# Field-pair projection: three stores a tile in place of four, five in the first tile and four in the last

## The chip, the cores and the metric

The kernel runs on one core of one Trainium2 chip. The time is that of one execution on the device, in microseconds (us). The kernel before took 684.77 us (median of three runs, 684.7 to 685.42).

## The reference

Every sample has 32 fields of 64 numbers. For each of the 496 pairs of fields (i, j) with i < j, field i is projected by the pair's own 64 x 64 matrix and multiplied, element by element, with field j:

```
r_x: (2048, 32, 64) float32      W: (496, 64, 64) float32
PAIRS = list(combinations(range(32), 2))
proj = einsum('bpd,pod->bpo', x[:, pi, :], W)
y    = proj * x[:, pj, :]        # (2048, 496, 64) float32
```

The output is 260 MB, the weights are 8 MB and x is 17 MB: it is above all a kernel that writes.

## The kernel before

The batch is cut into 16 tiles of 128 samples, one sample on each partition. The weights stay in SBUF from the start. For a tile, x is loaded into one of two buffers (`x_sb`), "turned" on TensorE (16 transposes into PSUM, which ScalarE copies to `x_t`), and then taken through 21 steps. A step has two halves (an even field i and an odd one), and each half is up to 1,024 columns, that is 16 pairs: TensorE multiplies the turned field with the weights into PSUM (`project`, line 294). Then VectorE multiplies PSUM with field j into the buffer `staged` (line 338). In the steps named in `pool_steps` (two of three) the second half goes another way: ScalarE copies PSUM into `staged` (line 260) and GpSimd multiplies it there with field j in place (line 221). PSUM holds two steps (`proj`, two buffers).

The steps of a tile form 11 groups of consecutive pairs: 61, 57, 53, 49, 45, 41, 37, 33, 54, 38 and 28 pairs. Groups 0 to 7 have two steps each (0 to 15), group 8 has steps 16 and 17, group 9 has 18 and 19, group 10 has step 20. The turn of the *next* tile's x stands between steps 9 and 10 (`TURN_BEFORE`); the last tile has none. `MERGED` says which groups share one *slot* of `staged` and one store. A slot exists once: the next tile may write into it when its store has landed. That is `slot_free` (line 163): VectorE waits ahead of the slot's first step, ScalarE ahead of the slot's first step with its work. All stores are issued by SyncE (SP), in order, each as soon as its last group is computed (lines 173 to 192); they run on queue q1, as do the loads of the weights and the first two x tiles. In the first and the last tile every group is stored by itself, 11 stores.

The x of tile t + 1 is loaded during tile t, by ScalarE's queue (q10): `load_x` (line 239) stands ahead of step 3 in ScalarE's order, behind the ScalarE copies of steps 0 and 1. It waits until all of tile t - 1 is computed, since that tile used the same buffer. TensorE waits for this load at the turn (line 302).

Each store writes one contiguous row per partition: 256 bytes a pair, so 30,208, 26,112, 31,488 and 39,168 bytes in the four stores of an inner tile. Sixteen DMA engines share the 128 partitions, 8 rows to each, and each engine ends a transfer with a small write to the semaphore. In the profile such a row is one packet.

Of the kernel before, what the change touches and what calls it, by code (L numbers as in the profile page):

```python
# [13 lines left out]
LOAD_BEFORE = 3  # L14
WARM_UP = 16

MERGED = [[0, 1], [2, 3], [4, 5, 6], [7, 8, 9, 10]]

DMA_SCRATCH = 1024

# [1 line left out]
def pair_index(i, j, fields):  # L22

    return i * (2 * fields - i - 1) // 2 + (j - i - 1)


def plan(fields, dim):


    fit = UNIT // dim  # L30
    steps, groups = [], []
    for i in range(0, fields // 2, 2):
        cut = fit if fields - 1 - i > fit + fit // 2 else fit // 2
        groups.append([len(steps), len(steps) + 1])
        steps.append(([(i, i + 1, cut)], [(i + 1, i + 2, cut)]))
        steps.append(([(i, i + 1 + cut, fields - 1 - i - cut)], [(i + 1, i + 2 + cut, fields - 2 - i - cut)]))

    def whole(*of):
        return [(i, i + 1, fields - 1 - i) for i in of]
    groups += [[len(steps), len(steps) + 1], [len(steps) + 2, len(steps) + 3], [len(steps) + 4]]  # L40
    steps += [(whole(16), whole(17)), (whole(18), whole(19)), (whole(20), whole(21)), (whole(22), whole(23)),
              (whole(24, 30, 26, 28), whole(25, 29, 27))]
    return steps, groups
# [30 lines left out]
def field_pair_project(nc, x, w, ident, out, fields, dim):  # L74
    batch = x.shape[0]
    tiles = batch // P
    steps, groups = plan(fields, dim)
# [10 lines left out]
    def items(tile):  # L88


        for n, item in enumerate(last_tile if tile.last else whole_tile):
            yield item, (1 + n) % 2, tile.number * per_tile + (1 + n) // 2
# [5 lines left out]
    def group_range(g):  # L98
        segments = [seg for s in groups[g] for unit in steps[s] for seg in unit]
        first = min(pair_index(i, j, fields) for i, j, _ in segments)  # L100
        assert sum(n for _, _, n in segments) == max(
            pair_index(i, j, fields) + n for i, j, n in segments) - first
        return first, sum(n for _, _, n in segments)


    slot_of = [next(k for k, merged in enumerate(MERGED) if g in merged) for g in range(len(groups))]
    slots = len(MERGED)
    slot_range = [(group_range(m[0])[0], sum(group_range(g)[1] for g in m)) for m in MERGED]


# [9 lines left out]
    def every_tile(emit):  # L120

        for t in range(tiles):
            emit(Tile(t, t % 2, t // 2, last=t == tiles - 1))
# [9 lines left out]
    with ExitStack() as ctx:  # L133
# [3 lines left out]
        def sem(name):  # L137
            return ctx.enter_context(nc.semaphore(name))
# [5 lines left out]
        x_t = [sb(f"x_t{h}", [P, fields // 2, P]) for h in range(2)]  # L144
        ident_sb = sb("ident_sb", [P, P])
        staged = [sb(f"staged{k}", [P, n * dim]) for k, (_, n) in enumerate(slot_range)]

        proj = [[ctx.enter_context(nc.psum_tensor(f"proj{b}{h}", [P, UNIT], F32)) for h in range(2)]
# [10 lines left out]
        stored = [sem(f"stored{k}") for k in range(slots)]  # L159
# [3 lines left out]
        def slot_free(eng, tile, k):  # L163

            if not tile.first:
                eng.wait_ge(stored[k], 16 * (tile.number + len(MERGED[k]) - 1))

        def staged_part(s, i, j, n):
            k = slot_of[group_of[s]]
# [3 lines left out]
        @block.sync  # L173
        def _(sp):
            def emit(tile):
                where = {item: (b, use) for item, b, use in items(tile)}
                fine = tile.first or tile.last
                for these in [[g] for g in range(len(groups))] if fine else MERGED:
                    k, g = slot_of[these[0]], these[-1]
                    first, n = group_range(these[0])[0], sum(group_range(h)[1] for h in these)  # L180


                    pooled = [h for h in these if any(s in pool_steps for s in groups[h])]
                    if pooled and these[0] == 0:
                        sp.wait_ge(pool_scaled[pooled[-1]], tile.number + 1)
                    b, use = where[groups[g][-1]]
                    sp.wait_ge(emptied[b][groups[g][-1] not in pool_steps], use + 1)
                    if pooled and these[0] > 0:
                        sp.wait_ge(pool_scaled[pooled[-1]], tile.number + 1)
                    at = (first - slot_range[k][0]) * dim  # L190
                    sp.dma_start(out[bass.ds(tile.number * P, P), first * dim:(first + n) * dim],
                                 staged[k][:, at:at + n * dim]).then_inc(stored[k], 16)

            half = fields * dim // 2
            sp.dma_start(x_sb[0][:, 0:half], x[0:P, 0:half]).then_inc(x_first_loaded[0], 16)  # L195
            sp.dma_start(w_sb[:, w_cuts[0]:w_cuts[1]], w[:, w_cuts[0]:w_cuts[1]]).then_inc(w_loaded[0], 16)  # L196
            sp.dma_start(x_sb[0][:, half:], x[0:P, half:]).then_inc(x_first_loaded[1], 16)  # L197
            for c in range(1, len(w_cuts) - 2):
                sp.dma_start(w_sb[:, w_cuts[c]:w_cuts[c + 1]], w[:, w_cuts[c]:w_cuts[c + 1]]  # L199
                             ).then_inc(w_loaded[c], 16)  # L200

            c = len(w_cuts) - 2
            sp.dma_start(w_sb[0:dim, w_cuts[c]:w_cuts[c + 1]], w[0:dim, w_cuts[c]:w_cuts[c + 1]]  # L203
                         ).then_inc(w_loaded[c], 16)
            sp.dma_start(x_sb[1][:], x[P:2 * P, :]).then_inc(x_loaded[1], 16)

            every_tile(emit)
            for k in range(slots):
                sp.wait_ge(stored[k], 16 * (tiles - 2 + 2 * len(MERGED[k])))

        @block.gpsimd
        def _(pool):
# [17 lines left out]
        def _(act):  # L230
# [17 lines left out]
            def emit(tile):  # L248
                for item, b, use in items(tile):
                    if item == LOAD_BEFORE and not tile.first and not tile.last:  # L250
                        load_x(tile)
                    if item == "turn":
                        turned_out(b, use, 1 - tile.parity)
                    elif item in pool_steps:
                        (i, j, n), = steps[item][1]
                        k = slot_of[group_of[item]]
                        if item == min(s for s in pool_steps if slot_of[group_of[s]] == k):
                            slot_free(act, tile, k)
                        act.wait_ge(filled[b][1], use + 1)  # L259
                        nc.scalar.activation(staged_part(item, i, j, n), proj[b][1][:, 0:n * dim],  # L260
                                             ACT.Copy).then_inc(emptied[b][1], 1)
# [58 lines left out]
        @block.vector  # L320
        def _(dve):
            def emit(tile):
                if tile.first:
                    for h in range(2):
                        dve.wait_ge(x_first_loaded[h], 16)
                for item, b, use in items(tile):
                    if item == "turn":
                        continue
                    k = slot_of[group_of[item]]
                    if item == groups[MERGED[k][0]][0]:  # L330
                        slot_free(dve, tile, k)
                    for h in range(2):
                        if h and item in pool_steps:
                            continue
                        dve.wait_ge(filled[b][h], use + 1)
                        segments = steps[item][h]
                        for (i, j, n), at in zip(segments, place(segments, dim)):
                            last = nc.vector.tensor_tensor(  # L338
                                staged_part(item, i, j, n), proj[b][h][:, at:at + n * dim],
                                x_sb[tile.parity][:, j * dim:(j + n) * dim], ALU.mult)  # L340
                        last.then_inc(emptied[b][h], 1)

            every_tile(emit)
# [31 lines left out]
```

## Time and profile before

| what | value |
|---|---|
| median of 3 runs | 684.77 us |
| the profiled execution | 684.55 us, span 682.7 us, mean granted clock 0.919 |
| busy: PE, DVE, ACT, POOL | 573.4, 409.3, 208.4, 391.9 us |
| HBM read, written | 24.97 MB, 260.05 MB: 417 GB/s over the span |
| stores | 14 each of 4896, 3936, 3776 and 3264 KB; 22 of 896 to 1952 KB |
| x loads on ScalarE's queue | 14 of 1024 KB, median 17.8 us to landing |
| chain that ended last | PE 55%, DMA 37% (all of it x loads) |

The page cuts the span into 40 slices of 17 us. The mean busy share of the 16 DMA engines is 90% or more in all of them but the first and the last; PE is at 90% or more in most, too, and none of its work is left in the last two slices. PE is TensorE, DVE is VectorE, ACT is ScalarE, POOL is GpSimd and SP is SyncE; "SPq" and "ACTq" are the queues from which the two issue DMAs. Times in rows count from the start of the span. A mean busy share can come out a little over 1, since a packet's time is counted where it starts.

### The profile page before, as it was taken

To read this page: it belongs to the slowest core of one execution; us is meant where nothing else is said; L and a number is where in the kernel's file an instruction comes from. 1 tells how busy PE (TensorE), PEld (TensorE's weight loads), DVE (VectorE), ACT (ScalarE), POOL (GpSimd) and SP (SyncE) were. 2 spreads that over 40 slices of the span, in tenths; PEclk is the share of its full clock that TensorE was granted. 3 is DMA by queue.
4 is the path that set the end of the run, shared out by engine and by line. 5 is a ranking of instruction groups with operands and counts; after the bars stand their busy time and mean duration, and the time that the engine had idled before them with its cause. 6 is when DMAs were issued, how large, how long until landed. Compare 5 with 4: busy or idle time off the path is not lost.

```text
span 682.7 us, 7003 instructions
## 1 busy us (share of the span) xinstructions
PE 573.4 (84%) x2704; PEld 363.3 (53%) x2704; DVE 409.3 (60%) x528; ACT 208.4 (31%) x257; POOL 391.9 (57%) x228
## 2 busy tenths in 40 slices
PE   6899989979799796988969889697996979979930
PEld 4565646546465564645646456464654646546520
DVE  1677775837567473764837638386583756837730
ACT  3334333323233333332323323233332323332300
POOL 1768674646566374674646836468464665647720
PEclk9999999989899898998989989899898989989975
DMA  8999999999999999999999999999999999999995
GB/s 336 386 426 425 439 438 423 434 436 428 432 432 431 432 428 436 435 427 428 431 427 429 428 404 410 428 421 407 426 426 424 422 415 429 399 439 419 421 421 233
DMA packets 15648, 285.20 MB, mean 418 GB/s; under 512 B 1744, under 2 KB 1872, under 8 KB 3856
## 3 DMA queue, kind: packets, MB, share of 16 engines
q1 hardware_dynamic: 13472, 270.28, 93.3%
q10 hardware_dynamic: 2160, 14.75, 5.1%
q8 instruction: 5, 0.08, 0.0%
q14 instruction: 11, 0.09, 0.0%
HBM read 24.97 MB, written 260.05 MB: 417 GB/s over the span
## 4 chain that ended last, share of the span: by engine, by line
PE 55%; DMA 37%; DVE 2%; SPq 1%; issue 1%; ACT 0%; DVEq 0%; ACTq 0%
PE proj L294 47%; DMA x_sb<-x_dram 37%; PE proj L272 7%; DVE staged L338 2%; SPq L199 1%; ACT staged L260 0%; SPq L203 0%; SPq L197 0%; SPq L196 0%; SPq L195 0%; DVEq L133 0%; ACTq L259 0%
## 5 line engine op out<-in xcount | busy, mean ns | idle before, releaser
L338 DVE TENSOR_TENSOR staged<-proj,x_sb 128x1024 f32<-128x1024 f32 (+7 forms) x528 | 409.3, 826 | 246.5 <-PE proj L294 210.8
L221 POOL TENSOR_TENSOR staged<-staged,x_sb 128x1024 f32<-128x1024 f32 (+4 forms) x224 | 391.7, 1755 | 261.4 <-ACT staged L260 258.4
L294 PE MATMUL proj<-w_sb,x_t 64*128 64x512 f32 (+7 forms) x2432 | 518.7, 533 | 3.6 <-DVE staged L338 2.1
L294 PEld LDWEIGHTS proj<-w_sb,x_t 64*128 64x128 f32 x2432 | 313.1, 188 | 204.3 <-issue 121.6
L260 ACT ACTIVATE staged<-proj 128x1024 f32<-128x1024 f32 (+4 forms) x224 | 174.6, 787 | 356.5 <-PE proj L294 329.1
L272 PE MATMUL proj<-ident_sb,x_sb 128*128 128x128 f32 x256 | 52.6, 390 | 71.2 <-DMA x_sb<-x_dram 71.2
L272 PEld LDWEIGHTS proj<-ident_sb,x_sb 128*128 128x128 f32 x256 | 47.1, 208 | 80.3 <-DMA x_sb<-x_dram 79.8
L236 ACT ACTIVATE x_t<-proj 128x1024 f32<-128x1024 f32 x32 | 32.5, 1024 | 86.2 <-PE proj L272 86.1
L311 PE MATMUL proj<-ident_sb 128*128 128x128 f32 x16 | 3.4, 405 | 5.6 <-DMA ident_sb<-ident_dram 5.6
L311 PEld LDWEIGHTS proj<-ident_sb 128*128 128x128 f32 x16 | 3.2, 223 | 5.6 <-DMA ident_sb<-ident_dram 5.6
L236 ACT ACT_TABLE_LOAD x1 | 1.3, 1283 | 1.2 <-PEq L368 1.2
L368 POOL MEMSET const-float32-0.0<- 128x1 f32 x1 | 0.1, 99 | 0.2 <-issue 0.2
L368 POOL MEMSET const-bfloat16-1.0<- 128x1 bf16 x1 | 0.1, 102 | 0.0
L368 POOL MEMSET const-uint8-127<- 128x1 uint8 x1 | 0.1, 102 | 0.0
L368 POOL MEMSET const-float32-1.0<- 128x1 f32 x1 | 0.1, 99 | 0.0
## 6 DMA issues: line engine op xcount, KB each, us to landing
out_dram<-staged SPq DMA_DIRECT2D x14, 4896.0 KB, 26.0
out_dram<-staged SPq DMA_DIRECT2D x14, 3936.0 KB, 23.0
out_dram<-staged SPq DMA_DIRECT2D x14, 3776.0 KB, 27.7
out_dram<-staged SPq DMA_DIRECT2D x14, 3264.0 KB, 27.7
x_sb<-x_dram ACTq DMA_DIRECT2D x14, 1024.0 KB, 17.8
out_dram<-staged SPq DMA_DIRECT2D x2, 1952.0 KB, 16.8
out_dram<-staged SPq DMA_DIRECT2D x2, 1824.0 KB, 20.6
out_dram<-staged SPq DMA_DIRECT2D x2, 1728.0 KB, 21.8
```

Of the source, the lines that this page charges most:

```text
L199: sp.dma_start(w_sb[:, w_cuts[c]:w_cuts[c + 1]], w[:, w_cuts[c]:w_cuts[c + 1]]).then_inc(w_loaded[c], 16)
L221: last = nc.gpsimd.tensor_tensor(product, product, x_sb[tile.parity][:, j * dim:(j + n) * dim], ALU.mult)
L236: nc.scalar.activation(x_t[to][:, h * (UNIT // P):(h + 1) * (UNIT // P), :].rearrange("p k b -> p (k b)"), proj[b][h][:], ACT.Copy).then_i ...
L260: nc.scalar.activation(staged_part(item, i, j, n), proj[b][1][:, 0:n * dim], ACT.Copy).then_inc(emptied[b][1], 1)
L272: last = nc.tensor.transpose(proj[b][h][:, n * P:(n + 1) * P], x_sb[of][:, k * P:(k + 1) * P], ident_sb[:])
L294: last = nc.tensor.matmul(proj[b][h][:, at:at + width], x_t[tile.parity][half, i // 2, :], w_sb[half, col:col + width], start=True, stop=True)
L311: nc.tensor.transpose(proj[1][0][:, 0:P], ident_sb[:], ident_sb[:])
L338: last = nc.vector.tensor_tensor(staged_part(item, i, j, n), proj[b][h][:, at:at + n * dim], x_sb[tile.parity][:, j * dim:(j + n) * dim], ...
L368: nc = bacc.Bacc("TRN2", target_bir_lowering=False, num_devices=1, dynamic_dma_scratch_size=DMA_SCRATCH)
```

## The change

Inner tiles are stored in three parts in place of four: groups 0 to 2 (171 pairs, 43,776 bytes a row), 3 to 6 (172 pairs, 44,032 bytes) and 7 to 10 (153 pairs, 39,168 bytes, as before). The slots of `staged` are cut in the same way, with the same size in sum. The first tile has five stores, of 61, 110, 94, 78 and 153 pairs. The last tile has four, of 171, 172, 87 and 66 pairs. The counts on the semaphores that say when a slot is free follow from how many stores of the first tile go to it. Steps, loads and their places in every engine's order stay.

```diff
-MERGED = [[0, 1], [2, 3], [4, 5, 6], [7, 8, 9, 10]]
+MERGED = [[0, 1, 2], [3, 4, 5, 6], [7, 8, 9, 10]]
+FIRST_MERGED = [[0], [1, 2], [3, 4], [5, 6], [7, 8, 9, 10]]
+LAST_MERGED = [[0, 1, 2], [3, 4, 5, 6], [7, 8], [9, 10]]
...
+    def stores_of(merged, k):
+
+        return sum(slot_of[these[0]] == k for these in merged)
+
...
             if not tile.first:
-                eng.wait_ge(stored[k], 16 * (tile.number + len(MERGED[k]) - 1))
+                eng.wait_ge(stored[k], 16 * (tile.number - 1 + stores_of(FIRST_MERGED, k)))
...
-                fine = tile.first or tile.last
-                for these in [[g] for g in range(len(groups))] if fine else MERGED:
+                for these in FIRST_MERGED if tile.first else LAST_MERGED if tile.last else MERGED:
...
             for k in range(slots):
-                sp.wait_ge(stored[k], 16 * (tiles - 2 + 2 * len(MERGED[k])))
+                sp.wait_ge(stored[k], 16 * (tiles - 2 + stores_of(FIRST_MERGED, k) + stores_of(LAST_MERGED, k)))
```

## Rows read from the trace of the kernel before

**Rows 1.** The page, DMA: packets and bytes; then q1's packets, MB, share.
```profile
DMA packets 15648, 285.20 MB, mean 418 GB/s; under 512 B 1744, under 2 KB 1872, under 8 KB 3856
...
q1 hardware_dynamic: 13472, 270.28, 93.3%
```

**Rows 2.** Windows: us; busy of PE, PEld, DVE, ACT, POOL; clock; DMA share, GB/s.
```profile
103.42:602.43 499.01, 431.92 (x2016) 273.83 (x2017) 306.76 (x396) 155.65 (x192) 293.80 (x168) 0.92 1.00 425
...
614.30:615.10 0.80, 0.80 (x8) 0.66 (x6) 0.02 (x2) 0.19 (x1) 0.54 (x1) 1.00 0.17 65
...
673.00:674.00 1.00, 0.00 (x0) 0.00 (x0) 0.00 (x0) 0.00 (x0) 0.00 (x0) 0.50 1.04 434
...
676.00:682.00 6.00, 0.00 (x0) 0.00 (x0) 0.00 (x0) 0.00 (x0) 0.00 (x0) 0.50 0.06 25
```

**Rows 3.** The chain of waits, in order of time: start, us, what.
```profile
103.42 2.95 PE proj L272 x16
...
143.69 3.67 PE proj L272 x16
...
309.98 3.68 PE proj L272 x16
...
318.33 9.19 PE proj L294 x36
...
520.37 3.67 PE proj L272 x16
...
561.26 3.67 PE proj L272 x16
...
584.59 17.79 DMA x_sb<-x_dram
...
602.43 3.67 PE proj L272 x16
...
609.67 9.19 PE proj L294 x36
```

**Rows 4.** Waits from 103.42 to 602.43: us in total, times, longest.
```profile
PE proj L272 <- DMA x_sb<-x_dram: 63.5, 12, 6.7
...
DVE staged L338 <- DMA out_dram<-staged: 29.7, 7, 5.6
```

**Rows 5.** DMA queues from 103.42 to 602.43: packets, MB, share of 16 engines.
```profile
q1 hardware_dynamic: 7055, 199.51, 93.7%
q10 hardware_dynamic: 1728, 12.58, 6.0%
```

**Rows 6.** Timeline of SP, ACT and POOL: start, us, engine, line, what, count.
```profile
52.83 0.33 ACTq L245 DMA_DIRECT2D x_sb<-x_dram  x1
...
573.21 0.33 SPq L191 DMA_DIRECT2D out_dram<-staged  x1
...
582.70 0.33 SPq L191 DMA_DIRECT2D out_dram<-staged  x1
...
590.26 0.33 SPq L191 DMA_DIRECT2D out_dram<-staged  x1
...
591.47 2.36 POOL L221 TENSOR_TENSOR staged<-staged,x_sb 128x1024 f32<-128x1024 f32 x1 [1.23 <-ACT staged L260]
...
593.46 1.02 ACT L260 ACTIVATE staged<-proj 128x1024 f32<-128x1024 f32 x1 [2.07 <-PE proj L294]
```

**Rows 7.** DMA queues from 592 to 596, amid an x load.
```profile
q1 hardware_dynamic: 32, 1.25, 79.3%
q10 hardware_dynamic: 32, 0.26, 15.5%
```

**Rows 8.** DMA queue q10 from 588 to 589.7 (none from 584.59 to 588).
```profile
q10 hardware_dynamic: 2, 0.02, 2.3%
```

**Rows 9.** DMA queue q1 from 597.5 to 601.5, the end of that x load.
```profile
q1 hardware_dynamic: 47, 1.44, 83.2%
```

**Rows 10.** The line of the x loads (L245), its 14 loads.
```profile
DMA to landing us min/median/max: 9.3/17.8/19.2
```

## The prediction

> **What bounds the kernel now.** I read the page's DMA lines first, because every engine has slack. They move 285 MB at a mean of 418 GB/s, and q1, with all the stores, holds them for 93.3% of the span [rows 1]. Then the windows: over the twelve inner tiles from 103.42 to 602.43 the mean share of the DMA engines is 1.00 at 425 GB/s, while TensorE (PE) is busy for 432 of 499 us [rows 2]. So the DMA engines are the wall. The end tells more. Up to 674 us all of them move data (434 GB/s), and from 676 to 682 the share is 0.06: one engine of sixteen is still at work, 7 us behind the others [rows 2]. All engines carry the same rows, so that engine is simply slower, and the run lasts as long as *its* rows last. It matters whether it ever pauses.
>
> The chain of waits shows the second limit. In every inner tile it goes from the x load (17.8 us) through the turn on PE and the later steps to the next x load [rows 3]. This loop took 41.17 us in the last inner tile and 41.03 a tile in the last two (602.43 - 520.37 = 82.06). 41.0 is also what I take as the slowest engine's own time for one tile, since it shows no pause before the end. In those late tiles the other fifteen already pause: in the 0.8 us from 614.30, behind the issue of a middle store, the share is 0.17 [rows 2]. PE waits for x 63.5 us in twelve tiles, against 29.7 us that VectorE waits for a store to free its slot [rows 4]. Two limits within 0.2 us of each other, then: the bytes, and the x loop. Anything that makes x later by more than that costs time.
>
> **The change, part by part.**
>
> *Fewer, longer rows.* A store sends one row per partition, 8 to each engine, and a semaphore write. Inner tiles go from 4 stores to 3 (14 fewer), the first tile from 11 to 5, the last from 11 to 4: 27 fewer, 27 x 9 = 243 packets of each engine's 978 (15,648 / 16) [rows 1]. What is one worth? q1 moved 199.51 MB in 93.7% of 16 x 499.01 us, 26.7 KB/us an engine; q10, with rows of 8,192 bytes, 12.58 MB in 6.0%, 26.3 KB/us [rows 5]. On 8,192 bytes that is 5 ns a packet: 243 x 5 ns = 1.2 us saved. Bounds: nothing below; above, if the slow engine's 7 us over its 978 packets were also a price per packet (7 ns more), 3.0 us. I take 1.2.
>
> *Slots.* Slot 0 now frees when the last of steps 0 to 5 has landed, slot 1 covers steps 6 to 13, slot 2 is as before. The slots' waits stand ahead of VectorE's and ScalarE's step, and behind them wait PE (two PSUM buffers) and the x load, which ScalarE issues ahead of step 3. Take one late tile. The middle store is issued at 573.21, the last at 582.70, x at 584.59 [rows 6]. A row of 172 pairs is 44,032 bytes, 1.65 us at 26.7 KB/us, so the new middle store lasts 13.2 us and lands some 15 us after 573.21, at about 588; its slot is wanted by step 6, which ScalarE copies at 593.46 [rows 6]. The first store (13.1 us) follows the last one and lands at about 617; its slot is wanted by step 0 of the next tile, just ahead of the next x issue, at about 624. Five us or more to spare: no wait. The first store becomes ready when GpSimd has finished step 4, 591.47 + 2.36 = 593.8 instead of 590.26 [rows 6]; the engines turn to it after the last store, at about 601. Covered by 7 us; without this cover each late us would be a pause.
>
> *The x load.* This is the part with a price. While x is loading, the engines take one row of a store, one row of x: between 592 and 596, 32 and 32 packets [rows 7]. So x, 8 rows an engine, lands after the 8 store rows that it is mixed with, and how long these are decides.
> The Trainium skill says the same in DMA: Bandwidth & Descriptors, section Queues, rings and completion order: an engine alternates between the queues' rings and drains a whole packet of one before it turns to the other. The trace agrees, and a packet here is one row.
> Now: the middle store (8 rows of 31,488) reaches the engines 0.8 us after its issue, then come 8 rows of 39,168. x is issued 11.38 us after the middle store; the engines take its first 2 rows between 588 and 589.7, 3.4 to 5.1 us after, and the others then [rows 3, 6, 8]. Hence it mixes with the second half of the last store and with 3 rows (30,208) of the next first store (47 packets of q1 on 16 engines, 1.44 MB) [rows 9], and lands 29.17 us after the middle store's issue (584.59 + 17.79 - 573.21). Bytes of stores ahead of x on one engine: 251.9 + 313.3 + 90.6 = 655.8 KB.
> After: the middle store starts at +0.8 and lasts 13.2, to +14.0; x's rows can begin at 11.38 + 3.5 = +14.9. So one row of the last store passes, x mixes with the other seven, and its eighth row follows that store's eighth; no row of the next store need pass. 352.3 + 313.3 = 665.6 KB, 9.8 KB more, 0.37 us. x lands at about 29.55. The step from the turn to the middle store's issue, 11.95 us (573.21 - 561.26), stays: the same steps 10 to 13. The loop becomes 41.5 us. It can be 1 us more where PE's granted clock is at its lower level for longer: turn and first matmuls took 8.35 us from 309.98 but 7.24 from 602.43 [rows 3].
> The slowest engine needs 41.0 for its rows. It falls behind by some 0.8 us a tile at first (the others made 40.27 from 103.42 to 143.69 [rows 3]), about 2 us in the first tiles, an estimate; that feeds it for some three of the 13 loads, and for the other ten it pauses 0.55 each (41.5 and the saved 0.05): 5.5 us. Bounds for the place of x: one row earlier (it slips in ahead of the last store, with 1.8 us less) the loop is 39.7 and costs nothing; one row later (a row of 43,776 passes before x's last) it is 43.1.
>
> *Tile 1.* The load there, issued at 52.83, takes 9.3 us [rows 6, 10], since it lies among rows of 8 to 14 KB. After the change the rows of 39,168 are on: 3.5 + 8 x (1.47 + 0.31) = 17.7, so the turn is at 70.5 and the middle store issued at 82.4. By then the engines have to move 33.1 MB (weights and three x tiles 11.3, tile 0 16.25, the first store 5.6), 79 us at 418 GB/s and a start of some 4: they are busy until 83. Cost none, but this cover is used up.
>
> *The end.* After the last turn no x load is in the way, and 821 pairs a partition remain from the middle store on, some 64 us on the slowest engine. Without a turn the last tile's steps run ahead of the engines, as now: from 673 to 674 PE is long idle and the engines are at 1.04 [rows 2]. Nothing lost.
>
> **Sum.** The profiled execution took 684.55 (span 682.7 and 1.85 around it), 0.22 below the median of 684.77. Median - 1.2 + 5.5 = 689.1; I say 689.0.
>
> **Rivals.** (1) *x slips in a row earlier.* Where the slow engine's lag at the middle store is between 0.3 and 2 us, x's first row passes ahead of the last store and the loop falls below the engine's 41.0. For it: the lag starts near 2, by the estimate above. Against: each tile whose loop is over 41.0 eats it. Time 684.8 - 1.2 = 683.6, with a few short pauses up to 686. (2) *Faster: packets cost more than I think.* The slow engine's lag is a price per packet, not per byte: 3.0 us saved, no pause, 681.8. It decides if a packet costs over 6 ns. For it: the rows give no other reason why one engine is slower. Against: 26.3 against 26.7 KB/us [rows 5] leaves no more than 5 ns on the average engine.
> The Trainium skill goes further in DMA: Bandwidth & Descriptors, section Anatomy of one DMA: about 2.0 us of fixed cost a transfer. By that alone 27 stores would be 54 us; it is an estimate from the page, and the share of 1.00 [rows 2] says that this cost lies beside other stores here (chance 0.01, within rival 2).
> (3) *x a row later.* Loop 43.1, 2.1 over 41.0, in 13 tiles 27 us: 711. Against: x's rows have 1 us to spare.
>
> **How the numbers follow.** Forecast 0.45 (686 to 697: 0.2 to 1.1 us a tile); rival 1 0.30; rival 2 0.12; rival 3 0.13. A measurement of this kernel can tell 0.2%, 1.4 us. Faster: rival 2 and a fifth of rival 1, 0.18. Same (683.4 to 686.1): the rest of rival 1 and a tenth of the forecast, 0.28. Slower 0.54. The range 681.5 to 699 leaves out rival 3 and half of rival 2.
>
> **What would show it.** Right: the x loads' median goes from 17.8 to 18 or more; the twelve turns lie over 41.3 us apart; the mean share over inner tiles falls below 1.00; the lonely engine's tail at the end shrinks from 7 us to 2 or less. The first x load takes about 17 us. Wrong: the tail stays and the turns lie 41.0 apart (rival 1), the DMA share stays 1.00 and the GB/s rise (rival 2), or the x loads take 20 us (rival 3). A wait of VectorE for a slot in every tile would break the part on slots.

## The result and the profile after

The changed kernel takes 709.81 us (median of six runs, 708.18 to 712.56); the kernel before, run beside it, 684.51 (683.84 to 685.42). The ratio is 1.0374, with a 95% interval of 1.035 to 1.0399: 25.3 us slower. Ratios here and below leave out executions over 1.5% above the fastest of the same kernel; only f1 and f3 had such, two of ten each. The forecast, 689.0, had the sign; the time lies outside its range and next to rival 3 (711).

The page after: packets of all queues; the x loads (KB, median us from issue to landing).

```profile
DMA packets 11760, 285.19 MB, mean 404 GB/s; under 512 B 1312, under 2 KB 1440, under 8 KB 3168
...
x_sb<-x_dram ACTq DMA_DIRECT2D x14, 1024.0 KB, 19.3
```

A quarter of the packets is gone [rows 1], and the mean rate fell from 418 to 404 GB/s: the engines pause. The windows after (columns as in rows 2) show where: the inner tiles first, then 2 us of a turn, the stretch just before a middle store's issue, and the end.

```profile
112.51:627.94 515.43, 432.06 (x2017) 273.11 (x2017) 308.31 (x396) 155.54 (x192) 293.60 (x168) 0.91 0.95 403
...
586.00:588.00 2.00, 2.00 (x11) 2.00 (x10) 0.00 (x0) 0.38 (x1) 0.00 (x0) 0.50 0.81 350
...
596.50:598.05 1.55, 1.55 (x10) 1.13 (x9) 0.77 (x3) 0.60 (x1) 1.23 (x2) 1.00 0.00 0
...
705.00:706.00 1.00, 0.00 (x0) 0.00 (x0) 0.00 (x0) 0.00 (x0) 0.00 (x0) 0.50 0.00 0
```

The share over inner tiles is 0.95 instead of 1.00 [rows 2], and in one 1.55 us stretch of a tile not a byte moves. The lone engine's tail is gone (0.00 from 705 to 706): in those pauses it catches up. The chain of waits (start, us, what) gives the loop:

```profile
52.12 17.94 DMA x_sb<-x_dram
...
70.10 3.47 PE proj L278 x16
...
112.51 3.68 PE proj L278 x16
...
608.63 19.26 DMA x_sb<-x_dram
...
627.94 3.67 PE proj L278 x16
```

Thirteen loops lie between the turns at 70.10 and 627.94: 557.84 / 13 = 42.91 us each. At 41.0, the slowest engine's own time a tile, the last turn would have been at 603.1 and the span 24.8 us shorter, 681.6. By this estimate the loops are the whole loss. The waits of PE's matmuls from 112 to 628 (us in total, times, longest) are for x, in each of the 13 turns there, but for 1.8 us; no engine waits for a store:

```profile
PE proj L278 <- DMA x_sb<-x_dram: 88.1, 13, 7.5
```

The issues of the last inner tile (timeline of SP and ACT): middle store, last store, x, next first store.

```profile
597.24 0.33 SPq L197 DMA_DIRECT2D out_dram<-staged  x1
...
606.74 0.33 SPq L197 DMA_DIRECT2D out_dram<-staged  x1
...
608.63 0.33 ACTq L251 DMA_DIRECT2D x_sb<-x_dram  x1
...
617.83 0.33 SPq L197 DMA_DIRECT2D out_dram<-staged  x1
```

So a loop is three terms: from the turn to the middle store's issue (A), from there to x's issue (11.39 in nearly every tile of both kernels), and x's load (L), with 0.04 us from landing to turn. Read off the chain as a mean of twelve loops each, the kernel before has A 12.2 and L 17.9, in all 499.01 / 12 = 41.58 [rows 2]; the kernel after, from 112.51, has A 12.2 (11.5 to 12.9) and L 19.3, in all 515.43 / 12 = 42.95. What the change adds to a loop, 1.4 us, is x's load alone.

### The profile page after: what moved, and what is told of

It is laid out like the page before. It is cut to its first block, busy times and chain, and to the rows that moved or that the text cites. A ratio compares the mean times of both kernels' runs of the same rounds, so it can differ in the third digit from the quotient of the medians.

```text
span 706.4 us, 6920 instructions
## 1 busy us (share of the span) xinstructions
PE 577.1 (82%) x2704; PEld 365.6 (52%) x2704; DVE 411.1 (58%) x528; ACT 208.5 (30%) x257; POOL 391.6 (55%) x228
## 4 chain that ended last, share of the span: by engine, by line
PE 52%; DMA 41%; DVE 1%; SPq 1%; issue 1%; ACT 0%; DVEq 0%
PE proj L300 45%; DMA x_sb<-x_dram 41%; PE proj L278 7%; DVE staged L344 1%; SPq L205 1%; SPq L209 0%; SPq L203 0%; SPq L202 0%; SPq L201 0%; ACT staged L266 0%; DVEq L140 0%
## 5 line engine op out<-in xcount | busy, mean ns | idle before, releaser
L278 PE MATMUL proj<-ident_sb,x_sb 128*128 128x128 f32 x256 | 55.0, 404 | 93.7 <-DMA x_sb<-x_dram 93.6
L278 PEld LDWEIGHTS proj<-ident_sb,x_sb 128*128 128x128 f32 x256 | 50.0, 218 | 102.9 <-DMA x_sb<-x_dram 102.9
## 6 DMA issues: line engine op xcount, KB each, us to landing
out_dram<-staged SPq DMA_DIRECT2D x15, 4896.0 KB, 19.3
x_sb<-x_dram ACTq DMA_DIRECT2D x14, 1024.0 KB, 19.3
out_dram<-staged SPq DMA_DIRECT2D x1, 3520.0 KB, 17.7
out_dram<-staged SPq DMA_DIRECT2D x1, 2496.0 KB, 17.9
```

Source lines behind the costliest of these rows:

```text
L278: last = nc.tensor.transpose(proj[b][h][:, n * P:(n + 1) * P], x_sb[of][:, k * P:(k + 1) * P], ident_sb[:])
```

## The experiments

**Which of the three edits?** The inner tiles alone, with 11 stores at both ends:

```
-FIRST_MERGED = [[0], [1, 2], [3, 4], [5, 6], [7, 8, 9, 10]]
-LAST_MERGED = [[0, 1, 2], [3, 4, 5, 6], [7, 8], [9, 10]]
+FIRST_MERGED = [[g] for g in range(11)]
+LAST_MERGED = [[g] for g in range(11)]
```

> Three stores in the inner tiles, eleven in the first and in the last tile, as before the change. If the inner x loop is the cause (x lands one store row later and the loop of an inner tile is 42.95 us in place of 41.0 to 41.2): 709 to 711 us, turns 42.9 apart. If the coarser first and last tile cost the time: 683 to 686 us.

Measured: 683.71, ratio 0.9989 (0.998 to 0.9999). The inner tiles with three stores cost nothing, and yet x loads as slowly as in the kernel after. Its chain:

```profile
496.16 19.74 DMA x_sb<-x_dram
...
515.95 1.97 PE proj L278 x16
...
537.51 19.22 DMA x_sb<-x_dram
...
556.77 1.97 PE proj L278 x16
```

L is 19.2 to 19.7, but the turn takes 1.97 us where the kernel after takes 3.3 to 3.7. PE's timeline shows why (last bracket: idle time ahead, and what ended it). This experiment:

```profile
510.94 4.70 PE L300 MATMUL proj<-w_sb,x_t 64*128 64x512 f32 x12 [4.46 <-DVE staged L344]
515.95 1.97 PE L278 MATMUL proj<-ident_sb,x_sb 128*128 128x128 f32 x16 [0.30 <-DMA x_sb<-x_dram]
```

and the kernel after:

```profile
585.62 3.42 PE L278 MATMUL proj<-ident_sb,x_sb 128*128 128x128 f32 x16 [6.72 <-DMA x_sb<-x_dram]
```

Both let PE stand idle once a tile. In the kernel after it is directly ahead of the turn, for x, and the granted clock is 0.50 (1.2 GHz) in the turn behind it. In e1 PE idles before the last 4.7 us of matmuls ahead of the turn, because VectorE waits for a store to free its slot, and by the turn the clock is back, in these windows of e1 (the turn's is the second):

```profile
508.00:510.00 2.00, 0.00 (x0) 0.00 (x0) 0.34 (x1) 0.34 (x1) 0.00 (x0) 0.53 0.99 422
...
516.00:518.00 2.00, 2.00 (x18) 1.83 (x20) 0.84 (x1) 1.58 (x3) 1.26 (x1) 1.00 0.86 370
```

The Trainium skill says in TensorE: Matmul & The Clock Gate, section Loop structure matters more than you think, that a loop which waits for a DMA ahead of its matmuls runs them cold. The trace agrees, 0.50 against 1.00.

The middle store behind the turn at 515.95 (timeline of SP):

```profile
526.12 0.33 SPq L197 DMA_DIRECT2D out_dram<-staged  x1
```

So A is 10.17 us instead of 12.2 (10.17 to 10.19 in all thirteen inner loops of e1), and 10.17 + 11.39 + 19.2 = 40.8, below the slowest engine's 41.0. The bytes bind (the span is 681.7 us, for the 681.6 worked out above), and the waits are for slots, where x cost only PE's line here (us, times, longest):

```profile
ACT staged L266 <- DMA out_dram<-staged: 134.9, 27, 6.1
DVE staged L344 <- DMA out_dram<-staged: 75.5, 24, 5.1
PE proj L278 <- DMA x_sb<-x_dram: 2.5, 5, 1.4
```

The ends alone, over the four slots of before (the lines against the kernel after):

```
-MERGED = [[0, 1, 2], [3, 4, 5, 6], [7, 8, 9, 10]]
-FIRST_MERGED = [[0], [1, 2], [3, 4], [5, 6], [7, 8, 9, 10]]
-LAST_MERGED = [[0, 1, 2], [3, 4, 5, 6], [7, 8], [9, 10]]
+MERGED = [[0, 1], [2, 3], [4, 5, 6], [7, 8, 9, 10]]
+FIRST_MERGED = [[0], [1], [2, 3], [4, 5, 6], [7, 8, 9, 10]]
+LAST_MERGED = [[0, 1], [2, 3], [4, 5, 6], [7, 8], [9, 10]]
```

> Four stores in the inner tiles as before; five in the first and five in the last tile (two groups to a store where the slot allows). If the inner loop is the cause: 683 to 685 us, the 12 stores fewer give at most 0.6 us. If the ends are the cause: over 700 us.

Measured: 684.7, 0.9997 (0.9987 to 1.0006). Its chain:

```profile
52.69 17.86 DMA x_sb<-x_dram
...
70.59 3.67 PE proj L278 x16
...
588.69 17.60 DMA x_sb<-x_dram
...
606.33 3.67 PE proj L278 x16
```

The first x load is as late as in the kernel after and the turns run at half clock to the end, at no cost, since x comes in 17.6. So neither edit is slow by itself; the loss is in their meeting.

**Is it x?** Every inner store as two DMAs, each of half the columns (`PARTS = 2`), so that rows are half as long; the counts on the semaphores follow:

```
+cuts = [n * c // parts(tile) for c in range(parts(tile) + 1)]
+for lo, hi in zip(cuts, cuts[1:]):
+    sp.dma_start(out[bass.ds(tile.number * P, P), (first + lo) * dim:(first + hi) * dim],
+                 staged[k][:, at + lo * dim:at + hi * dim]).then_inc(stored[k], 16)
```

> The changed kernel, slots, waits and points of issue the same, but every inner store is issued as two transfers of half the columns, so its rows are 19.6 to 22 KB in place of 39 to 44 KB. If the length of the rows that x alternates with is what makes it late: x loads of 13 to 15 us in place of 19.3, turns 40.0 to 41.2 apart, 670 to 686 us. If it is the merging itself (slots free later, the middle store can be issued only after the turn): x loads may shorten but the time stays at 705 to 711 us. If packets or transfers cost much by themselves: slower than 711 us.

Measured: 685.46, 1.0011 (1.0001 to 1.002); the x loads take 13.6 us at the median, for 19.3. And x issued by SP ahead of the tile's last store, so that it shares q1 and passes nothing (`load_x` is taken out of ScalarE's order):

```
+if these[-1] == len(groups) - 1 and tile.number + 2 < tiles:
+    sp.dma_start(x_sb[tile.parity][:], x[bass.ds((tile.number + 2) * P, P), :]
+                 ).then_inc(x_loaded[tile.parity], 16)
```

> The changed kernel with the x loads issued by SyncE on the stores' own queue, directly ahead of the last store of a tile, under the same condition. In one queue x does not alternate with rows: it follows the middle store and comes ahead of the last one. By the x theory x lands about 17 us after the middle store's issue in place of 30.6, PE does not wait for it, and the bytes alone set the time: 668 to 685 us. If the idle time of the DMA engines comes from three slots being too few, it stays over 700 us.

Measured: 684.23, 0.9991 (0.998 to 1.0001); PE waits for x once, 0.6 us. Either way of making x early takes all, or nearly all, of the loss away.

**Which end?** The kernel after with 11 stores in the first tile only, then in the last tile only:

```
+FIRST_MERGED = [[g] for g in range(11)]      (first of the two)
+LAST_MERGED = [[g] for g in range(11)]       (second)
```

> The changed kernel with eleven stores in the first tile alone; inner tiles three, last tile four. Theory of two states: in tile 1 the x load lies among short rows again, PE does not idle ahead of its first turn, the turn runs at the full clock, and the loop of an inner tile stays at 40.8 us, below the 41.0 of the slowest DMA engine: 683 to 685 us. Rival, the coarse last tile has a part in it: 690 us or more.

> The changed kernel with eleven stores in the last tile alone; first tile five, inner tiles three. Theory of two states: the loop comes into the slow state in tile 1 as with the change, turns 42.9 us apart, 707 to 711 us. Rival, the last tile matters: 683 to 690 us.

Measured: 683.94, 0.9987 (0.9977 to 0.9998), and 710.52, 1.0388 (1.0363 to 1.0413). The last tile has no part in it. In the first tile, x of tile 2 could be what matters, or something else that the coarse stores delay. So only that one load of fourteen was moved, to SP, ahead of the first tile's last store:

```
+if tile.first and these[-1] == len(groups) - 1:
+    sp.dma_start(x_sb[0][:], x[bass.ds(2 * P, P), :]).then_inc(x_loaded[0], 16)
...
-if item == LOAD_BEFORE and not tile.first and not tile.last:
+if item == LOAD_BEFORE and 1 < tile.number < tiles - 1:
```

> The changed kernel with one load of 14 moved: the x load of tile 1 is issued by SyncE on the stores' queue, just ahead of the first tile's last store; all others as they are. Theory of two states: that load lands some 10 us earlier, PE meets its first turn without a pause, and all later tiles stay in the fast state: 683 to 686 us. Rival, five stores in the first tile cost through their slots or every long x load costs its share: 700 to 711 us, since 13 of 14 loads are as before.

Measured: 683.43, 0.9981 (0.9971 to 0.9991). One load, early, saves 26 us over the next thirteen tiles, though the later ones still take 19.3 us at the median. Call a loop early when its turn runs at full clock (A 10.17) and late when it runs at half clock. The early loop can be lost on the way; f3's chain in the execution of 683.51 us shows it near the end:

```profile
517.72 1.97 PE proj L280 x16
...
558.60 3.46 PE proj L280 x16
...
600.95 3.67 PE proj L280 x16
```

There the half clock behind PE's wait for a slot lasted into the turn (0.50 from 553 to 557, and 0.50 from 558.60 to 560.60), and the next loop took 42.35. Of ten executions each, two of f1 (698.14 and 703.55 us) and two of f3 (704.61 and 705.24) were far longer at the same code. That they lost the early loop sooner is argued from their times; they have no trace. The opposite, e1 with only tile 1's load ahead of step 8 in place of step 3:

```
-if item == LOAD_BEFORE and not tile.first and not tile.last:
+if item == (8 if tile.number == 1 else LOAD_BEFORE) and not tile.first and not tile.last:
```

> The kernel with three stores in the inner tiles and eleven at both ends (683.7 us), with one load changed: in tile 1 x is loaded ahead of step 8 in place of step 3. Theory of two regimes: PE idles ahead of the first turn, the turn runs at half clock, and the run stays in the slow regime for all later tiles: 705 to 712 us. Rival, a late first load costs once and is made up from the stores in the queues: 684 to 692 us.

Measured: 715.04, 1.0444 (1.0426 to 1.0461). One load, late, and twelve tiles on the chain still reads as in the kernel after:

```profile
594.38 3.49 PE proj L278 x16
...
617.48 19.25 DMA x_sb<-x_dram
...
636.77 3.68 PE proj L278 x16
```

With x loaded ahead of step 3, the inner code thus has two loops, and whichever it enters in tile 1 it mostly keeps.

**Is it the clock?** If half clock behind the idle time carries the late loop, work for PE in that time must break it. Idle transposes ahead of each turn, 24 and then 52:

```
 if item == "turn":
+    if not tile.first:
+        pe.wait_ge(emptied[b][0], use)
+        for _ in range(KEEP_WARM):
+            nc.tensor.transpose(proj[b][0][:, 0:P], ident_sb[:], ident_sb[:])
```

> The changed kernel with 24 more transposes of the identity on PE ahead of each turn from tile 1 on (5 us at the full clock, written to the PSUM part that the turn writes next, so no result of theirs is used). If the half clock at the turn is what holds the loop at 42.9 us: the turn takes 1.97 us in place of 3.67, turn to middle store's issue 10.2 in place of 12.3, loop 40.8 to 41.2, 684 to 690 us. Rival, the x load's length alone sets the loop: 705 us or more, and slower still if the transposes get in the way.

> As the run with 24 transposes ahead of the turn, but 52 of them: the 24 took only 2.84 us, 4 us of idle time were left ahead of x and the turn still ran at half clock (3.68 us), so that run did not test the clock. 52 take 6.1 us of the 6.7 to 7.4. If the half clock is what holds the loop at 42.9: turn 1.97 us, turn to middle store 10.2, loop 40.8 to 41.2, 683 to 690 us. If the x load's length alone sets it: 705 us or more.

With 24: 709.76, 1.038 (1.0353 to 1.0406). PE's timeline there shows that this did not test the clock: they last 2.84 us, four idle microseconds remain, and but for the first turn (1.96 us at 70.25) the turns are as slow as ever.

```profile
578.72 2.84 PE L312 MATMUL proj<-ident_sb 128*128 128x128 f32 x24
585.55 3.38 PE L279 MATMUL proj<-ident_sb,x_sb 128*128 128x128 f32 x16 [3.99 <-DMA x_sb<-x_dram]
```

With 52: 686.73, 1.0037 (1.0023 to 1.0052). PE's timeline again, then the chain:

```profile
558.63 5.90 PE L312 MATMUL proj<-ident_sb 128*128 128x128 f32 x52
564.38 1.97 PE L279 MATMUL proj<-ident_sb,x_sb 128*128 128x128 f32 x16
```

```profile
362.04 1.97 PE proj L279 x16
...
383.60 19.26 DMA x_sb<-x_dram
...
402.91 1.97 PE proj L279 x16
```

The turn runs at full clock, x takes 19.26 as in the kernel after, and the loop is 40.87 as in e1. The mean granted clock is 0.979, for 0.909 in the kernel after. Of the 25.3 us 23.1 are back, with added work on PE and without touching a byte or a DMA. So the clock is a link that the late loop can't do without.

**The same stores with x a little earlier.** If x's lateness is what starts it, x earlier by a step or two should be enough:

```
-LOAD_BEFORE = 3
+LOAD_BEFORE = 1
```

> The changed kernel with the x load ahead of step 1 in ScalarE's order in place of step 3, so that it is issued up to 1.9 us sooner. If x came one store row too late (its rows began 5.7 us after the issue, behind two rows of the last store, where I had counted one), it now goes one row earlier: x lands 1.6 to 1.9 us sooner after the middle store's issue, the loop falls to 41.0 or just above, 683 to 695 us. If the rows' place does not matter: 705 to 712 us.

Measured: 683.31, 0.9983 (0.9973 to 0.9994), and all ten executions between 682.82 and 685.49: the loss is gone, and the kernel before is matched, or beaten by 0.2%. x is issued together with the last store or up to 0.7 us behind it, instead of 1.89. Its chain:

```profile
106.29 3.67 PE proj L278 x16
...
394.80 3.68 PE proj L278 x16
...
434.99 1.97 PE proj L278 x16
...
597.83 1.92 PE proj L278 x16
```

It starts in the late loop too (half clock from 106.29), but at 288.51 / 7 = 41.2 us a tile that costs next to nothing, and from 434.99 on it is in the early one. What brought it there is not shown.

**Can more be had?** With x out of the way the slowest DMA engine's 41.0 a tile is the bound. Each x load dealt as transfers of 120 and 8 partitions, on top of e4, was to take rows off that engine:

```
+for lo, n_rows in ((0, 120), (120, 8)):
+    sp.dma_start(x_sb[tile.parity][lo:lo + n_rows, :],
+                 x[bass.ds((tile.number + 2) * P + lo, n_rows), :]
+                 ).then_inc(x_loaded[tile.parity], 16)
```

> The kernel with the x loads on the stores' queue (684.2 us), where one DMA engine, 41.0 us a tile, sets the time. Each x load is issued as two transfers, of 120 and of 8 partitions, which the engines share out in another way, 15 and 8 of them. If the slow engine is one that gets less by it: up to 2 us a tile less on it, the others' 40.0 to 40.3 take over, 668 to 676 us. If the slow engine is one that gets a ninth row: 686 to 690 us. If no engine is slow by itself: 684 us.

Measured: 692.92, 1.012 (1.0103 to 1.0137), so the guess of the engine was wrong, or the deal was: 8.7 us more than e4. Which engine it is stays open.

## Why the prediction was wrong

*What failed: the place of x's rows, "x's rows can begin at 11.38 + 3.5 = +14.9", so that "no row of the next store need pass".* Two DMA queue views, of 608.63 to 614.3 and of 614.3 to 625 (packets, MB, share), and one of the end, 625.7 to 627.4:

```profile
q1 hardware_dynamic: 64, 1.96, 85.3%
```

```profile
q1 hardware_dynamic: 96, 3.76, 83.7%
q10 hardware_dynamic: 96, 0.79, 17.4%
```

```profile
q1 hardware_dynamic: 22, 0.96, 130.9%
q10 hardware_dynamic: 7, 0.00, 0.2%
```

The first view has no q10 at all: x's rows began 5.7 us behind their issue, not 3.5, and so two rows of the last store passed, not one. In the second view rows go one for one, 96 and 96, as the prediction had it. In the third, x's data are through (0.00 MB on q10), and only its closing small writes are left, behind a row of the next first store on each engine (0.96 MB / 22 = 43.6 KB a packet), which was to have been out of x's way. From the middle store's issue to x's landing it took 608.63 + 19.26 - 597.24 = 30.65 us; the step said 29.55. That is the place of rival 3, against which the text held "1 us to spare". That rival 3's 711 came so near is in part luck: its row was to make x 1.6 us later, and x was 1.1 later. Why the first row came after two and not after one was not settled.

*"The step from the turn to the middle store's issue, 11.95 us, stays."* It stayed, but 11.95 was that of one late tile. Over the twelve inner tiles of the kernel before it lies between 11.7 and 13.1; between this turn and the next x issue lie 24.49 us, that is A 13.10:

```profile
395.09 3.68 PE proj L272 x16
...
419.58 17.92 DMA x_sb<-x_dram
```

The mean is 12.2 before and after, 0.3 more than was put in. With the 1.1 of x's place this is the loop: 42.95 for the 41.5 predicted. The prediction had named the clock here ("It can be 1 us more") and put it at nothing in the sum.

*"That feeds it for some three of the 13 loads."* It fed none: all 13 loops are over 41.0 (42.2 to 44.1). Priced again with what was measured: 13 x 1.95 = 25.3, against 10 x 0.55. Of the 20 us missed, 10 x 1.4 are the loop's size and 3 x 1.95 these three loads.

*"Cost none, but this cover is used up" (tile 1).* The numbers held (load 17.94 for 17.7, turn 70.10 for 70.5), but the verdict failed worst. I took the loop's length as a sum of fixed terms, and A is not fixed: it is 10.2, or 12.2 on the mean, by whether the turn runs at full or at half clock. Late x makes PE idle there, the clock fall, the middle store late and with it the next x: a loop of 42.95 that feeds itself, where the same stores in step run at 40.8 and leave the bytes as the bound. f1, f3 and g3 show that tile 1's load decides between them, g1 that the clock holds the late one up. The kernel before ran late as well (turns of 3.67 [rows 3]), but with the shorter L its loop was 41.58 on the mean, only 0.6 over the slowest engine's 41.0, and the share of 1.00 [rows 2] says that stores already waiting in the queue covered that.

*What held.* No wait for a slot in the kernel after. x's loads longer, the DMA share below 1.00, the turns over 41.3 apart, the tail gone: all as listed. The coarse last tile cost nothing (e2, f2); the coarse first tile cost nothing by itself either (e2), but with the coarse inner tiles it brings on the loss (f1). Packets: 27 stores fewer were priced at 1.2 us. By their intervals e1, with 14 fewer, saves 0.9 (0.1 to 1.4), f3 and g2, with all 27 fewer and x moved, 1.3 (0.6 to 2.0) and 1.2 (0.4 to 1.9), and e2, with 12 fewer in the ends, nothing that can be told from zero. That fits the 1.2, though no run changes the packets alone. Rival 2 is out; no run gained 3 us. Nothing like the 54 us shows that the prediction works out from the Trainium skill's 2.0 us a transfer; the section named there, Anatomy of one DMA in DMA: Bandwidth & Descriptors, gives that figure for transfers issued by GpSimd, and SyncE issues these.

## What to carry to other kernels

Where a loop closes within a per cent of the bandwidth bound, write it as a sum of terms, take each as a mean over tiles and not from one, and ask of each whether it depends on where the idle time falls; here one late load at the start chose the longer loop for the whole run. Longer rows saved about 1 us here, where the engines were busy throughout (a share of 1.00), and they delayed the small load on the other queue by whole rows. Issue the load that closes the loop early, or on the stores' own queue ahead of them, before making the stores coarser.

## What the hardware showed that I had not expected

The same inner code on one core runs at 40.8 or 42.95 us a tile, and one load of fourteen chooses which (f3, g3). One DMA engine of sixteen needs about 41.0 us a tile where the others need about 40: in the trace of the kernel before, the first completion of a tile's last store comes every 40.0 us from 109.9 to 309.8, and the sixteenth falls behind the fifteenth from 0.35 us to 4.4. With pauses in the loop this no longer shows, and which engine it is no run told. Identity transposes back to back behind warm matmuls took 2.84 / 24 = 0.118 us each.
